# Slot dispatch: the weights stream through TensorE, are divided ahead of their transposes, and all queues are put in a new order

## The reference, cut to what matters

```python
x = L0_attn_x                                     # 32 batches, 256 tokens, 128 features
x = x + _layernorm(_L0_attn_ref(_layernorm(x), Wq, bq, Wk, bk, Wv, bv, Wo, bo))
x = x + _layernorm(_L0_ffn_ref(_layernorm(x), gamma_x, gamma_slot, slot_embeds, w1, w2))

# _L0_attn_ref: causal linear attention, 16 heads of 8
q, k = exp(q), exp(k)
kv, k1 = cumsum(k[..., None] * v[..., None, :], 1), cumsum(k, 1)
out = einsum('zsD,zsDd->zsd', q, kv) / sum(q * k1)
...
# _L0_ffn_ref: soft mixture, 8 experts x 64 slots = 512 slots
logits = einsum('bsd,etd->bset', xn, se)
dispatch = softmax(logits, axis=1)                # over the tokens, for each slot
slots = einsum('bsd,bset->betd', xn, dispatch)
h = gelu(slots @ w1)                              # 128 -> 512
processed = h @ w2                                # 512 -> 128
combine = softmax(logits over all 512 slots)      # for each token
out = einsum('bnd,bsn->bsd', processed, combine)
```

## Time and profile before

| | |
|---|---|
| median of 3 runs | 635.28 us (634.94 to 636.53) |
| the profiled execution's span, first to last instruction | 633.3 us |
| PE busy | 583.9 us, 92% |
| PEld busy | 515.1 us, 81% |
| DVE busy | 475.3 us, 75% |
| ACT busy | 438.2 us, 69% |
| POOL busy | 481.5 us, 76% |
| granted TensorE clock, mean | 0.996 of full speed |
| DMA, mean | 23 GB/s |

### The profile page before, as it was taken

How to read it: one execution, slowest core, us unless ns; L and a number is a source line. 1 busy time by engine, 2 the same in 40 slices (tenths; PEclk the granted TensorE clock), 3 DMA queues, 4 the chain that set the end, 5 groups by cost and what they waited for, 6 DMA issues and landing times.

```text
span 633.3 us, 11705 instructions
## 1 busy us (share of the span) xinstructions
PE 583.9 (92%) x4136; PEld 515.1 (81%) x4136; DVE 475.3 (75%) x922; ACT 438.2 (69%) x1087; POOL 481.5 (76%) x495
## 2 busy tenths in 40 slices
PE   3456999999999999999999999999999999999886
PEld 2344888888898888888988888898988888888875
DVE  5978687887777788877777888777778788767521
ACT  4135677777777777777777777777777777777755
POOL 5878788888888888888888888888888888873100
PEclk9999999999999999999999999999999999999999
DMA  3000001000000000000000000000000000000000
GB/s 100 17 18 18 18 9 33 10 26 26 26 26 26 21 22 16 21 26 25 26 26 26 18 18 18 26 26 26 26 26 19 25 9 26 18 18 9 9 9 18
DMA packets 16829, 14.35 MB, mean 23 GB/s; under 512 B 2850, under 2 KB 16644, under 8 KB 16772
## 3 DMA queue, kind: packets, MB, share of 16 engines
q1 hardware_dynamic: 14708, 12.76, 6.7%
q10 hardware_dynamic: 2064, 0.86, 0.5%
HBM read 5.25 MB, written 4.19 MB: 15 GB/s over the span
## 4 chain that ended last, share of the span: by engine, by line
PE 51%; DVE 23%; ACT 18%; issue 4%; POOL 2%; DMA 1%; SPq 0%; DVEq 0%; POOLq 0%; ACTq 0%
PE HB L912 16%; DVE WB L1170 12%; PE LA L889 9%; ACT L477 6%; PE LA L868 5%; ACT comb L597 5%; PE WB L750 3%; PE WB L840 3%; ACT slT_hi L474 2%; PE LB L878 2%; DVE xnT_lo L1127 2%; DVE att L1180 2%; PE WB L791 2%; ACT xnT_hi L474 2%; PE WB L824 2%
## 5 line engine op out<-in xcount | busy, mean ns | idle before, releaser
L912 PE MATMUL HB<-w_c,hid 128*128 128x128 f32 x992 | 120.7, 275 | 0.5 <-ACT hid L481 0.5
L912 PEld LDWEIGHTS HB<-w_c,hid 128*128 128x128 f32 x992 | 117.3, 192 | 0.7 <-ACT hid L481 0.7
L481 ACT ACTIVATE hid<-HB 128x512 f32<-128x512 f32 x128 | 76.6, 599 | 32.1 <-PE HB L752 26.1
L1155 DVE TENSOR_TENSOR prod<-WB,E 128x768 f32<-128x768 f32 x96 | 90.9, 948 | 5.3 <-PE WB L841 5.1
L214 POOL TENSOR_TENSOR kv<-E 128x1024 f32<-128x1024 f32 x32 | 68.4, 2136 | 33.4 <-ACT E L474 33.4
L1170 DVE TENSOR_REDUCE WB<-prod 128x288 f32<-128x2304 f32 x32 | 81.9, 2561 | 3.1
L338 POOL TENSOR_TENSOR kv_lo<-kv,kv_hi 128x1152 fp32r<-128x1152 f32 x31 | 82.3, 2656 | 2.5
L398 POOL TENSOR_TENSOR kv<-kv,kv_prev 128x1024 f32<-128x1024 f32 x31 | 74.1, 2390 | 0.0
L214 POOL TENSOR_TENSOR kv_prev<-prev 128x1024 f32<-128x1024 f32 x31 | 66.2, 2136 | 2.6 <-DMA prev<-E 2.6
L925 PE MATMUL LA<-proc,comb 128*128 128x129 f32 x512 | 62.6, 274 | 1.5 <-ACT proc L474 1.5
L889 PE MATMUL LA<-xn,disp 128*128 128x129 f32 x512 | 62.6, 275 | 0.5 <-ACT disp L474 0.4
(11 more groups left out here) (143 smaller groups left out, 1517.9 us busy)
## 6 DMA issues: line engine op xcount, KB each, us to landing
X<-in_L_attn_x_dram SPq DMA_DIRECT2D x32, 128.0 KB, 2.2
out_dram<-res SPq DMA_DIRECT2D x32, 128.0 KB, 1.8
prev<-E SPq DMA_DIRECT2D x32, 112.0 KB, 2.1
w_in<-in_L_ffn_w_dram ACTq DMA_DIRECT2D x2, 256.0 KB, 4.5
prev<-E SPq DMA_DIRECT2D x32, 15.0 KB, 2.0
se_in<-n_L_ffn_slot_embeds_dram ACTq DMA_DIRECT2D x1, 256.0 KB, 3.6
w_in<-in_L_attn_Wq_dram SPq DMA_DIRECT2D x1, 64.0 KB, 2.2
w_in<-in_L_attn_Wk_dram SPq DMA_DIRECT2D x1, 64.0 KB, 2.2
```

The costliest lines, as they stand in the source:

```text
L481: act.activation(hid[:, f, :], HB[:, f % 2, :], ACT.Gelu).then_inc(gelu_ready[f], 1)
L912: last = pe.matmul(PR[:, j, :], hid[:, f, j * P:(j + 1) * P], w2_c[:, f, :], start=(f == 0), stop=(f == FJ - 1))
L1155: dve.tensor_tensor(prod[u][:, :, d0 * DIM:d1 * DIM].rearrange("p c (d f) -> p c d f", d=g), WB[:, k % 2, 0:g * DIM].rearrange("p (o d f) ...
```

## The change

It has three parts. (1) The gather has `xn` as the stationary operand and `disp` as the moving one, 512 columns wide, and writes the slots already transposed into HB; the column of ones, `slots_scale` and `slots_transpose` are gone. (2) The sums that divide the softmax come from accumulators of `dispatch_exp` (one per slot tile), and VectorE divides `disp_t` in place, 128x1024 numbers, ahead of the transposes. (3) The orders of all five queues are new, and operations are cut finer: `project`, `hidden`, `dispatch_transpose`, `dispatch_copy`, `combine_exp` are called by halves, the keys' sum is apart from `outer_odd` (`pair_keys`). ScalarE's Gelu table is loaded behind `xnT_high`. The special forms of the last batch (`process_last`, `PR_last`, the loading of the exponential's table ahead of time) are gone. Waits that another wait already implies are left out.

```diff
-        xn = [sb(f"xn{u}", [P, NC, YW]) for u in range(2)]
+        xn = [sb(f"xn{u}", [P, NC, DIM]) for u in range(2)]
+        disp_sum = sb("disp_sum", [P, SJ])
-        slots = sb("slots", [P, SJ, DIM])
...
             def dispatch_exp(n):
-                    last = act.activation(disp_t[:, j, :], LBv[:, j, :], ACT.Exp, bias=neg_max[:, j:j + 1])
+                    last = act.activation(disp_t[:, j, :], LBv[:, j, :], ACT.Exp, bias=neg_max[:, j:j + 1], accum_out=disp_sum[:, j:j + 1])
...
+            def dispatch_scale(n):
+                dve.wait_ge(disp_exp, n + 1)
+                dve.reciprocal(disp_inv[:, :], disp_sum[:, :]).then_inc(disp_inverted, 1)
+                dve.wait_ge(disp_inverted, n + 1)
+                dve.tensor_tensor(disp_t[:, :, :], disp_t[:, :, :],
+                                  disp_inv[:, :].rearrange("p (j o) -> p j o", o=1).broadcast_to((P, SJ, SEQ)),
+                                  ALU.mult).then_inc(disp_scaled, 1)
...
             def gather_slots(n):
-                for c in range(NC):
-                    after(pe, disp_ready[c], n)
-                for j in range(SJ):
-                    for c in range(NC):
-                        last = pe.matmul(SL[:, j // 2, j % 2, :], disp[:, c, j * P:(j + 1) * P], xn[n % 2][:, c, :],
-                                         start=(c == 0), stop=(c == NC - 1))
-                last.then_inc(slots_done, 1)
-
-            def slots_transpose(n):
-                after(pe, slots_ready, n)
-                after(pe, proc_ready, n - 1)
-                for j in range(SJ):
-                    last = pe.transpose(HB[:, 0, j * P:(j + 1) * P], slots[:, j, :], ident[:, :])
-                last.then_inc(slT_done, 1)
+                pe.wait_ge(disp_ready[0], n + 1)
+                for c in range(NC):
+                    last = pe.matmul(HB[:, 0, :], xn[n % 2][:, c, :], disp[:, c, :], start=(c == 0), stop=(c == NC - 1))
+                last.then_inc(slT_done, 1)
...
             def load(n):
-                after(sp, x1_ready, n - NX)
+                after(sp, x1_ready, n - 4)
...
+            def step(s):
+                load(s)
+                shift_odd(s - 2)
+                store(s - 8)
```

More of the change, by code:

```diff
@@ L187, in attention_and_slot_mixture @@
[L187 to L194, removed]
@@ L450, in first_steps @@
[L450 to L464 removed]
+                slot_norms()
+                own_value(0)
@@ new lines, in first_steps, with step @@
+                own_product(1)
+                outer_odd(1)
+                outer_even(1)
+                pair_keys(1)
+                pair_sum(1)
+            def step(s):
+                x_rstd_of(s)
+                o_rstd_of(s - 6)
+                sums_high(s - 2)
+                sums_low(s - 2)
+                y_rstd_of(s - 3)
+                own_value(s - 2)
+                own_product(s - 1)
+                x_negative(s - 2)
+                x1_rstd_of(s - 3)
+                outer_odd(s - 1)
+                outer_even(s - 1)
+                pair_keys(s - 1)
+                pair_sum(s - 1)
@@ L467, in last_steps @@
                 o_rstd_of(31)
-            pipeline(pool, first_steps, step, last_steps)
+            first_steps()
+            for s in range(3, 32):
+                step(s)
+            last_steps()
         @block.scalar
@@ L725, in _ @@
             copy(wqkv_hi[:, :], LB[:, 0, 0:QKV]).then_inc(s_wqkvhi, 1)
-            pipeline(act, first_steps, step, last_steps)
+            first_steps()
+            for s in range(3, 32):
+                step(s)
+            last_steps()
         @block.tensor
@@ L1041, in _ @@
+                process(31, 1)
+                mixture(31)
+            first_steps()
+            for s in range(7, 32):
+                step(s)
+            last_steps()
         @block.vector
@@ new lines, in first_steps @@
+                attention(3)
+                xT_low(5)
+                slot_maxima(2)
+                part_maxima(2)
+                second_residual(0)
+                token_maxima(2)
+                own_sum(4)
+                dispatch_scale(2)
+                first_residual(3)
+                multiply(4, 0)
+                multiply(4, 1)
+                x_normalise(6)
+                x1_normalise(3)
+                multiply(4, 2)
+                x_statistics(7)
+                slT_low(2)
@@ L1350 @@
+                second_residual(31)
+            first_steps()
+            for s in range(8, 29):
+                step(s)
+            last_steps()
 _INS = ["L0_attn_x", "L0_attn_Wq", "L0_attn_bq", "L0_attn_Wk", "L0_attn_bk", "L0_attn_Wv", "L0_attn_bv",
```

1439 lines of the change are left out of this document (786 added, 653 removed).

## The result

The changed kernel took 683.73 us (median of 4 runs, 680.89 to 690.53), the kernel before 635.54 on the same chip; the ratio is 1.0771, with an interval of 1.0712 to 1.0829. The profiled run has a span of 683.9 us. The forecast was 664 with a range of 618 to 672: the side is right, the size is not. Where executions of one kernel lie over 1.5% apart, as those of `e9_guard_alone` do, only the faster ones are compared.

What follows compares the result with a forecast made beforehand. Bound before: TensorE nearly full, plus a loop through ScalarE and VectorE; after, a GpSimd loop of 19.2 us. 24 steps at 1.23 us more give 29.5; 633.3 + 29.5 = 662.8, median 2.0 above: 664 us, range 618 to 672.

Steps and rivals of the forecast that it cites:

- TensorE is not the bound; the gather gains nothing, the slots' transposes go: TensorE: its own work falls from some 17.3 us a step to 16.8; gather gains 0.05, slots' transposes about 0.5.
- rival (c): Gather on TensorE: the weight load binds and the gather halves; with (a) 614 us, its chance counted within (a)'s 0.27.
- The divided softmax: weights divided at 6.44, T = 17.3 alone: Loop through exponentials, division and TensorE: weights divided 6.44 us after the attention transpose, period T 17.3, gain 0.65 a step.
- 10.8 in the sum: TensorE: 10.8 us from the start of the dispatch transposes to the next attention transpose, where it was 13.07.
- The loop through x1, the shift and GpSimd: 3.2 + 12.6 + 3.4 = 19.2: Period: 3.2 us x1 to outer product, 12.6 GpSimd to end of `sums_low`, 3.4 on to the next x1.
- 662.8 and 2.0: Total: profiled span 633.3 + 29.5 = 662.8 us; the median of the runs lies 2.0 above the span.
- Here it turns: SyncE's new order: the shift stands behind a load that waits for x1, so GpSimd's outer product waits 3.2 us.
- TensorE idle ahead of the dispatch transposes by 2 us: Sign that the forecast is right: TensorE waits 2 us there in the middle of the profile after.
- Rival (d): `x1_normalise` is caught by GpSimd's outer product too: 2 us more on VectorE, 672 us and more; chance 0.06 with worse.
- (a): `x_normalise` meets no long GpSimd instruction, or at little cost: period 17.3 us, total 619, 615 to 624; chance 0.27.
- (b): `x_normalise` slips through, but the product holds GpSimd's `y_rstd_of`: period 18.1 us, about 640; chance 0.15.
- The upper end, 672: Top of the range 618 to 672 us; the forecast's own was 653 to 671, from 18.8 to 19.4 a step.

Runs made afterwards that it cites:

- e9_guard_alone: Changed kernel, with GpSimd's outer_odd(n) waiting until x1_normalise(n-2) is done and the last outer_odd ahead of outer_even: 670.75 us profiled, 681.67 to 684.08 in three others.
- e7_outer_waits: e6_halves with the shift issued ahead of the load and outer_odd(n) waiting until x1_normalise(n-2) is done: 610.82 us, ratio 0.9594.
- e12_fill_guard: e9_guard_alone with ten more TensorE transposes a step, in the wait for the division: 658.97 us, ratio 1.0364.
- e6_halves: e1_xh_late with the last shifts waiting for x1, the last outer_odd ahead of outer_even, and the division's product in two halves: 618.84 us, ratio 0.9726.
- e1_xh_late: Changed kernel with x_normalise(s) moved from behind part_maxima(s-4) to behind first_residual(s-3): 641.97 us, ratio 1.0098.
- e2_shift_first: Changed kernel with SyncE's order alone undone, the shift of batch s-2 issued ahead of the load of batch s: 736.12 us, ratio 1.1574.

## Why the prediction was right on the side and wrong on the size

**TensorE is not the bound; the gather gains nothing, the slots' transposes go.** Right. Four gather matmuls take 1.83 us in the chain of `e7_outer_waits`, 0.04 more than the sixteen of the earlier trace rows; the work is the width, and rival (c) is out. The ground that I gave, 0.6 ns between groups of 128 and of 129 columns, was thin for it.

**The divided softmax: weights divided at 6.44, T = 17.3 alone.** Right. From the first exponential to the divided weights I had 3.52 us; in the short step above they start at 422.31 and the product ends at 425.72, 3.41. With nothing in the way and the product in halves the period is 17.27. With the product in one piece the short steps of the changed kernel have 17.77, of which 11.44 us (10.8 in the sum) lie behind the transposes: TensorE waits 0.40 there for the copy of the dispatch weights.

**The loop through x1, the shift and GpSimd: 3.2 + 12.6 + 3.4 = 19.2.** Right, to a tenth, once the clock is out of it. In `e12_fill_guard` x1 is ready at 204.04, the outer product starts at 207.21 (3.17), `kv_lo` ends at 219.79 (12.58), and x1 had been ready 3.31 behind the `kv_lo` ahead of it (ended at 200.73): 19.06, measured 19.07. The changed kernel without the lower clock takes 663.4, the forecast was 664. So close a hit in the total has luck in it: the 663.4 hold the two long xn pairs at the end, which the sum did not have (`e12_fill_guard`, without them, takes 659.0), and 662.8 and 2.0 are 664.8, not 664.

**What I made of it: "Here it turns", said of SyncE's order.** Half wrong. The 3.2 us are in the loop, but to take them out makes the kernel 52 us slower, since they are also what keeps the outer products off `x1_normalise`. I had put `x1_normalise` "0.2 us ahead of the outer product" and did not ask who decides that. The margin that a transfer gives was in the sum as a cost alone.

**"TensorE idle ahead of the dispatch transposes by 2 us".** The wait was forecast and its price was taken as its length. This is the step that failed. I reckoned 10.8 us from the transposes to the next attention transpose, at the full clock, which is what the steps with the clock at 1.0 show (10.72). Behind most of these waits the clock falls, and the stretch takes 12.25; where the second meeting follows, it mostly takes 14.8 and the step 23.1 in place of 19.2. In the earlier trace rows there is no such step, as TensorE had no wait of that length in the loop before.

**Rival (d), `x1_normalise` caught as well: "2 us more on VectorE, of which most is covered", 0.06.** It happened in ten steps, from the middle on in every second. In nine of them the clock had fallen ahead of it (in three more it fell and the pair was not caught), and with the waits filled eight of the ten are free of it; the last two, at batches 28 and 29, stay. So the clock started it in those eight, and not 0.2 us in the phases. Its price as a separate thing was not settled (between nothing and 13 us). So 0.06 was too little for the case; the 20 us between forecast and measurement come from the clock together with what it starts.

**The chances.** (a), no meeting, 17.3 us a step and 619, did not happen by itself; `e6_halves` (17.50, 618.8) and `e7_outer_waits` (17.27, 610.8) reach it. (b) is `e1_xh_late`. The upper end, 672, was drawn from the loop alone. It should have had what the lower clock behind TensorE's wait costs.

## What to carry to other kernels

Where VectorE and GpSimd both work from SBUF to SBUF, list for each of VectorE's such instructions which long instruction of GpSimd can have started just before it, and who decides the order: a transfer that happens to be late is a guard, and if it goes, an explicit wait has to take its place. A wait that is forecast for TensorE can be dearer than its length, as the work behind it may run at the lower clock. Filler work in the wait tells in one run whether it does; it gave 20 us here, while `e7_outer_waits`, in whose loop TensorE has no such wait, is 73 faster (683.7 to 610.8). And a long instruction on one of the two engines can be worth cutting up (the product in halves gave 16 us, `kv_lo` in four 32, the clock's share included).

## What the runs showed of the hardware

- TensorE had a mean granted clock of 0.58 to 0.59 for some 4 us behind single waits of 2.0 to 2.3 us, in the changed kernel's step above after 5.5 us without a gap; behind others of up to 2.37 us it kept 1.00. Ten more transposes in each wait made the changed kernel 20 us faster (683.7 to 663.4).
- In a meeting VectorE waits again for each of its instructions, when GpSimd's next one stands ready: a pair took 4.22 us in `e2_shift_first`, one outer product for each of the two. GpSimd had started 0.07 us ahead.
- VectorE's instructions with one side in PSUM did not take part: in the two steps of the changed kernel shown above, a maximum (1.22) ran beside `kv_hi` and a multiply (0.93) beside the outer product at their usual times.
- An accumulator on an exponential of 256 columns costs 0.09 us from start to start (0.45 beside 0.36).
